# Cross attention: weighed values turned by VectorE in blocks, projections issued in halves, and another split of the copies from PSUM

## What is computed

```python
x = _layernorm(x + _L0_xattn_ref(x, mask_Bx1xSxS_fk0, ctx_2048, L0_xattn_Wq, L0_xattn_Wk, L0_xattn_Wv, L0_xattn_Wo, L0_xattn_gate), axis=-1)
...
q = split_heads(hidden_states @ Wq, q_len)
k = split_heads(hidden_states @ Wk, q_len)
v = split_heads(hidden_states @ Wv, q_len)
...
q = q * cos + _rotate_half(q) * sin
k = k * cos + _rotate_half(k) * sin
scores = jnp.einsum('bhqd,bhkd->bhqk', q, k) * inv_sqrt_d
scores = scores + attention_mask
...
attn_output = jnp.einsum('bhqk,bhkd->bhqd', w, v)
...
a_scores = jnp.tanh(gate) * jax.nn.softmax(a_scores.astype(jnp.float32), axis=-1).astype(q.dtype)
attn_output = attn_output + jnp.einsum('bhqk,bhkd->bhqd', a_scores, a_v)
attn_output = attn_output.transpose(0, 2, 1, 3).reshape(bsz, q_len, hid)
return attn_output @ Wo
```

## Time and profile before

| | |
|---|---|
| three runs, us | 2973.5, 2974.13, 2975.09 (median 2974.13) |
| the profiled execution | 2976.63 us, its span 2974.8 us |
| cross-attention loop | 1713.1 to about 2747 us of the span |
| busy: TensorE, VectorE, ScalarE | 94%, 59%, 47% of the span |
| moved by DMA | 100.10 MB, mean 34 GB/s |

### The profile page before, as it was taken

One profiled execution on the slowest core, in us unless ns is written; L12 is line 12 of the kernel. 1 busy time (PEld: TensorE's weight loads), 2 busy tenths in 40 slices (PEclk: granted clock), 3 DMA queues, 4 the chain that ended last, 5 costly groups with the idle time before them and its releaser, 6 DMA issues. The chain is left out here.

```text
span 2974.8 us, 81892 instructions
## 1 busy us (share of the span) xinstructions
PE 2807.7 (94%) x34646; PEld 1760.9 (59%) x34646; DVE 1748.0 (59%) x4940; ACT 1384.1 (47%) x3313; POOL 503.5 (17%) x626
## 2 busy tenths in 40 slices
...
...
DMA packets 96922, 100.10 MB, mean 34 GB/s; under 512 B 38192, under 2 KB 84528, under 8 KB 95408
## 3 DMA queue, kind: packets, MB, share of 16 engines
...
## 5 line engine op out<-in xcount | busy, mean ns | idle before, releaser
L201 PE MATMUL dr_p<-x_t,dr_w_g 128*128 128x512 f32 x1536 | 740.1, 609 | 11.0 <-DMA dr_w_g<-in_w_in 7.6
L1276 ACT ACTIVATE xa_probs<-xa_probs,xa_low 128x256 f32<-128x256 f32 x1024 | 436.6, 497 | 45.6 <-DVE xa_low L1428 43.6
L201 PEld LDWEIGHTS dr_p<-x_t,dr_w_g 128*128 128x128 f32 x1536 | 268.2, 191 | 226.5 <-issue 216.4
L1428 DVE CUSTOM_DVE_ANT_0 xa_probs<-xa_s,xa_mask 128x256 f32<-128x256 f32 x512 | 213.8, 418 | 263.0 <-PE xa_s L1187 263.0
L1200 PEld LDWEIGHTS xa_t<-ident,xa_probs 128*128 128x128 f32 x2048 | 223.2, 142 | 132.2 <-issue 79.1
L635 DVE SCALAR_TENSOR_TENSOR dr_acc<-dr_p,dr_taps,dr_acc 128x510 f32<-128x510 f32 (+2 forms) x384 | 284.9, 742 | 23.2 <-ACT dr_acc L493 15.2
L1200 PE MATMUL xa_t<-ident,xa_probs 128*128 128x128 f32 x2048 | 286.9, 281 | 7.7 <-DVE xa_probs_t L1437 6.0
L1282 ACT ACTIVATE xa_probs_t<-xa_t 128x512 f32<-128x512 f32 x256 | 152.8, 597 | 250.7 <-PE xa_t L1200 249.1
L1428 DVE CUSTOM_DVE_ANT_0 xa_probs<-xa_s,xa_zeros 128x256 f32<-128x256 f32 x512 | 214.4, 419 | 0.0
L1437 DVE COPY xa_probs_t<-xa_t 128x512 f32<-128x512 f32 x256 | 176.3, 689 | 43.4 <-PE xa_t L1200 29.4
L1215 PE MATMUL xa_o<-xa_probs_t,xa_val 128*32 128x128 f32 x4096 | 140.7, 278 | 44.6 <-DVE xa_probs_t L1437 24.8
...
...
...
## 6 DMA issues: line engine op xcount, KB each, us to landing
...
```

The lines of the kernel that those rows point to most:

```text
L201: mm = pe.matmul(bank[:, :], w_g[:, k, m, :], x_t[:, k, 2 * S * batch:2 * S * (batch + 1)], start=(k == 0), stop=(k == KC - 1))
L1276: op = act.activation(at, at, ACT.Exp, bias=low[:, v % 3, i, kind:kind + 1], scale=-1.0)
L1428: op = dve.tensor_tensor_reduce(out=probs[:, v % 3, i, kind, :], in0=bank_s[i][:, kind * S:(kind + 1) * S], in1=mask[:, par, q, :] if kind ...
```

## The change

norm and turn are no longer pieces of TensorE, and mixed is no longer copied by ScalarE. In each even unit VectorE transposes bank_o (128x512) in blocks of 32x32 into mixed (*turn_mixed*, after the first two tops), which brings 32 queries of each of four head pairs to the rows; it shares out as before, now from SBUF into *joined*, and transposes that (128x128) in blocks into attn_t, the layout that out reads (*share*, at the end of the unit). attn_t has two slots.

The pieces stand in two tables: BETWEEN (between the halves) and BEHIND (behind both). The ten pieces of HALF are issued in two parts, half of their matmuls at one place and half at the next; the bank is waited for at the first part only, and taken after the last. ScalarE copies both bank_t after the first half of turn_probs, VectorE both after the second, each ahead of what followed the copies before. The root moves to unit 7 of a batch, the rate to unit 8. The gate is laid out for the new rows. The diff, cut:

```diff
-        attn = a.sb("attn", [P, 2, D])
-        attn_t = a.sb("attn_t", [P, KC, P])
+        joined = a.sb("joined", [P, 4, 2, XD])
+        attn_t = a.sb("attn_t", [P, 2, XT, P])
...
-        copied = [sem(f"copied{j}") for j in range(2)]
+        copied = [[sem(f"copied{m}{j}") for j in range(2)] for m in range(2)]
...
-        LATE = {0: "x0", 1: "x1", 2: "q0", 3: "q1", 5: "qt0", 6: "ak0", 7: "ak1", 8: "k0", 9: "k1", 10: "v0", 11: "v1",
-                12: "av0", 13: "av1"}
-        EARLY = {7: "qt1", 11: "kt0", 13: "kt1"}
...
+        HALF = {"ak0", "ak1", "q0", "q1", "v0", "v1", "k0", "k1", "av0", "av1", "out0", "out1"}
+        BETWEEN = ("ak0", "ak1", "x0", "count", "q0", "q1", "out1", "qt1", "v0", "v1", "k0", "k1", "av0", "kt1", "av1", "out0")
+        BEHIND = ("ak0", "ak1", "x1", "q0", "q1", "qt0", "out1", "v0", "v1", "k0", "k1", "kt0", "av0", "av1", "spread", "out0")
...
-            if d % 2 == 0:
-                return ("norm", u // 2 - 1) if u else None
-            if d == 9:
-                return "turn", QT * b
-            if d == 1:
-                return ("turn", QT * b - 1) if b else None
-            if d == 15:
-                return ("spread", b - 1) if b else None
-            if d == 3:
-                return ("count", b - 2) if b > 1 else None
-            return (EARLY[d], b + 1) if d in EARLY and b + 1 < B else None
...
+            what = (BEHIND if behind else BETWEEN)[d]
+            use = named(what, b)
+            if not use:
+                return None
+            if what not in HALF:
+                return use, True, True
+            whole = list(itertools.chain.from_iterable(zip(BETWEEN, BEHIND)))
+            is_first = whole.index(what) == 2 * d + behind
+            return use, is_first, not is_first
...
-        BY_DVE = ("qt0", "qt1", "kt0", "kt1", "norm", "out", "count")
+        BY_DVE = ("qt0", "qt1", "kt0", "kt1", "out", "count")
...
-            wait_taken(pe, previous[use])
...
+            if first:
+                wait_taken(pe, previous[use])
...
-                for h in range(2):
+                for h in halves_now:
...
-            elif what == "norm":
-                wait(pe, mixed_taken, at + 1)
-                for n in range(4):
-                    mm = pe.transpose(bank[:, n * P:(n + 1) * P], mixed[:, n * P:(n + 1) * P], ident)
-            elif what == "turn":
-                wait(pe, normed, XT * (at + 1))
-                for k in range(KC):
-                    mm = pe.transpose(bank[:, k * P:(k + 1) * P], attn[:, at % 2, k * P:(k + 1) * P], ident)
...
-                wait_taken(pe, ("turn", at))
-                for k in range(KC):
-                    mm = pe.matmul(bank[:, :], attn_t[:, k, :], w_o[:, k, :], start=(k == 0), stop=(k == KC - 1))
-            mm.then_inc(made, 1)
+                wait(pe, normed, XT * (at + 1))
+                for k in quarters_now:
+                    mm = pe.matmul(bank[:, :], attn_t[:, at % 2, k, :], w_o[:, k, :], start=(k == 0), stop=(k == KC - 1))
+            if last:
+                mm.then_inc(made, 1)
...
-                    if i == 2 and inner(v):
-                        pe_make(pe, inner(v))
+                    if i == 2 and piece(v, 0):
+                        pe_make(pe, *piece(v, 0))
                     wait(pe, exped, 4 * v + i + 1)
-                    wait(pe, copied[i % 2], 2 * v + i // 2)
+                    wait(pe, copied[1 - i // 2][i % 2], v + i // 2)
...
-                if outer(u):
-                    pe_make(pe, outer(u))
+                if piece(u, 1):
+                    pe_make(pe, *piece(u, 1))
...
-            def copy(v, m):
-                wait(act, turned[0], 2 * v + m + 1)
+            def copy(v):
...
-                act.activation(probs_t[:, v % 2, 2 * m].rearrange("p k t n -> p (k t n)"), bank_t[0][:, :], ACT.Copy)\
-                    .then_inc(copied[0], 1)
+                for j in range(2):
+                    wait(act, turned[j], 2 * v + 1)
+                    act.activation(probs_t[:, v % 2, j].rearrange("p k t n -> p (k t n)"), bank_t[j][:, :], ACT.Copy)\
+                        .then_inc(copied[0][j], 1)
...
-                copy(u, 0)
-                if early(u):
-                    act_take(act, early(u))
-                copy(u, 1)
+                copy(u)
+                if ended(u, 0):
+                    act_take(act, ended(u, 0))
                 if u + 1 < LAST:
                     exps(u + 1)
-                if late(u):
-                    act_take(act, late(u))
-                if u % HALVES == 5 and u > HALVES:
+                if ended(u, 1):
+                    act_take(act, ended(u, 1))
+                if u % HALVES == 7 and u > HALVES:
...
-                if u % 2:
-                    g = u // 2
-                    wait(act, weighed, 8 * (g + 1))
-                    if g:
-                        wait(act, made, made_at["norm", g - 1])
-                    act.activation(mixed[:, :], bank_o[:, :], ACT.Copy).then_inc(mixed_taken, 1)
...
+        def turn_mixed(v, g):
+
+            wait(v, weighed, 8 * (g + 1))
+            v.transpose(mixed[:, :], bank_o[:, :]).then_inc(mixed_taken, 1)
+
...
+            for h in range(2):
+                op = v.reciprocal(shares[:, :, h], blocks[:, :, h, :, 1 - h, 0])
...
+            v.tensor_tensor(shares[:, 1], shares[:, 1], gains[:, t, :, None].to_broadcast([P, 2, 4]), ALU.mult).then_inc(norm_step, 1)
...
+            op.then_inc(norm_step, 1)
+            wait(v, norm_step, 4 * g + 3)
+            v.tensor_tensor(joined[:].rearrange("p q h d -> p h q d"), parts[:, 0], parts[:, 1], ALU.add).then_inc(norm_step, 1)
+            if t == 0 and tile >= 2:
+                wait(v, made, made_at["out", tile - 2])
+            wait(v, norm_step, 4 * g + 4)
+            v.transpose(attn_t[:, tile % 2, t, :], joined[:].rearrange("p q h d -> p (q h d)")).then_inc(normed, 1)
...
-            def copy(v, m):
-                wait(dve, turned[1], 2 * v + m + 1)
+            def copy(v):
...
-                dve.tensor_copy(probs_t[:, v % 2, 2 * m + 1].rearrange("p k t n -> p (k t n)"), bank_t[1][:, :]).then_inc(copied[1], 1)
+                for j in range(2):
+                    wait(dve, turned[j], 2 * v + 2)
+                    dve.tensor_copy(probs_t[:, v % 2, 2 + j].rearrange("p k t n -> p (k t n)"), bank_t[j][:, :]).then_inc(copied[1][j], 1)
...
-                    tops(u + 1, 0)
-                copy(u, 0)
-                if early(u):
-                    dve_take(dve, early(u))
-                if u + 1 < LAST:
-                    tops(u + 1, 1)
-                copy(u, 1)
+                    tops(u + 1, 0, 1)
+                if u and u % 2 == 0:
+                    turn_mixed(dve, u // 2 - 1)
+                if ended(u, 0):
+                    dve_take(dve, ended(u, 0))
+                copy(u)
...
-                if late(u):
-                    dve_take(dve, late(u))
-                if u % HALVES == 6 and u > HALVES:
+                if ended(u, 1):
+                    dve_take(dve, ended(u, 1))
+                if u and u % 2 == 0:
+                    share(dve, u // 2 - 1)
+                if u % HALVES == 8 and u > HALVES:
...
+            turn_mixed(dve, LAST // 2 - 1)
+            share(dve, LAST // 2 - 1)
```

89 lines of the change are left out of this document (42 added, 47 removed).

## The result

| | before | after |
|---|---|---|
| four runs each, us | 2971.02 to 2975.09, median 2973.82 | 2886.79 to 2895.5, median 2894.46 |
| ratio, with its 95% interval | | 0.9726 (0.9714 to 0.9738) |
| the profiled execution | 2976.63, span 2974.8 | 2894.66, span 2892.8 |
| mean granted clock of TensorE | 0.982 | 0.981 |

The kernel is 79 us faster. 2888 was forecast, with 2862 to 2926 around it, so the forecast is 6.5 us too low.

A forecast was written before the change was run, and what follows sets the result against it. TensorE was taken to bound the kernel, with 11.3 us of stalls a batch. Gains of 75.6 (seven batches), 9.7 (last batch) and 1.3 (tail) made 86.6: 2976.6 to 2890.0, less 2.5 for the runs' median, 2888; range 2862 to 2926.

The forecast's parts named there:

- The batch, 117.1: Sixteen units of a full batch: 116.3 us plus 0.8 for joints of split pieces, down from 127.9; 75.6 over seven batches.
- The walk: Unit-by-unit reckoning of a full batch: 3.94 us fixed TensorE work plus pieces, later where VectorE or ScalarE is late.
- Ten pieces leave TensorE: 5.1 us: Per batch, eight norm and two turn pieces leave TensorE, 0.51 us each: 5.1 us.
- Unit 6 near 7.6 in place of 10.1: Unit 6 of a batch loses norm's 1.33 us wait on ScalarE's copy mixed, falling from 10.13 to 7.57 us.
- The copies: ScalarE copies both banks after the first half, VectorE after the second; split pieces hide them; light units take 5.8 us.
- The last batch: 9.7 forecast: Last batch, nearly all light units: eight even units gain about 1 us each, the table-change unit some more.
- fewer stalls give it no new cause to fall; I count nothing: TensorE's granted clock, read as 1.00 in batch 5 and two units, stays there: no time counted.
- The tail: 1.3 less forecast: After the last batch, choose ends at 2726.03 as before and the last out starts at 2728.3, not 2729.58.
- Rival A: VectorE's PSUM transpose runs at half pace, 1.4 us not 0.65: 33 us less gain, 2921; chance 0.17.
- Rival B: The walk's own stalls, 4.8 us a batch, vanish as VectorE works ahead in heavy units: 2865; chance 0.09.
- C: VectorE becomes the bound: at 6 us more a pair of units, 128 us slower, 3100; chance 0.03.
- D: Gain undone, within 0.2%: light units wait behind ScalarE's second copy as long as before behind VectorE's; chance 0.03.

The follow-up runs named there:

- turned_twice: The changed kernel with the 128x512 block transpose from PSUM made twice, the first into a scratch tile: 2903.83 us, ratio 0.9774 to the kernel before.
- turn_alone: The changed kernel with VectorE turning and root and rate moved, but pieces whole in their old places and the old copies: 2948.94 us, 0.9932.
- gap_filled: turn_alone with four unread transposes put back where norm stood, in even units with a whole piece behind: 2950.53 us, 0.9918.
- busy_in_wait: The changed kernel with 24 unread TensorE transposes ahead of the weighing in units 0 and 9 of the last batch: 2890.61 us, 0.9725.
- spread_router: The changed kernel with VectorE's choose and rate cut and moved across units, and last values turned ahead of choose: 2886.39 us, 0.9711.

## Why the prediction was right, and where its sizes were off

**TensorE bounds the kernel, with its stalls around it: right.** All that moved the units did so through TensorE's issue, its waits or its clock. VectorE could take 44 us more for some 10 (turned_twice).

**The batch, 117.1: measured 116.67**, so 78.7 for seven batches where 75.6 were forecast. The walk's numbers for the pieces, taken from start to start in the earlier trace rows, hold to a tenth of a microsecond. Unit 0 is half a microsecond longer than forecast: VectorE takes out0, issued in unit 15, and its statistics ahead of choose, which begins 1.14 us after the scores (2183.95 against 2182.81) and not 0.8. Units 1 and 9 are 0.3 and 0.16 shorter, and the 0.8 for the joints is not there: units 1 to 15 last 108.38 together, the walk without it has 108.37. VectorE's busy time rose by 5.4 us a batch and not by 8.

**"Ten pieces leave TensorE: 5.1 us".** As a difference of issue it is right, as a gain it was not one of itself. With the old places (turn_alone) the turning and the moved root and rate give 2.1 us between two full batches (127.9 to 125.8), and four transposes in norm's gap cost nothing (gap_filled). The prediction counted the whole batch anew and so didn't fall into this, but a sum of "removed instructions by duration" would have. The other 59 us come with the new places. Whether the places without the turning would have done it wasn't tried: norm needs the one bank_p between the halves of a split piece.

**Unit 6 near 7.6 in place of 10.1: right in its size** (7.67), by a chain that was read one link short. Norm waited for ScalarE's copy "mixed", but that copy was late because the root stood ahead of it and loaded another table. From ScalarE's timeline of the kernel before:

```profile
2275.02 1.28 ACT L1268 ACT_TABLE_LOAD   x1
...
2276.52 0.58 ACT L1309 ACTIVATE xa_mixed<-xa_o 128x512 f32<-128x512 f32 x1
```

In the first batch, which has no root (and no out before it), unit 6 took 8.79. The change takes the copy off ScalarE and moves the root to unit 7 as well; no run divides the two. In its new place the root costs nothing in a full batch (unit 8 takes 7.49 to 7.50, with it and without it).

**The copies.** That ScalarE's and VectorE's new order is what hides the waits was the forecast's reading; the runs don't bear it out. Swapped back it makes no difference on the old places (2949 and 2950), little on the new ones (2890 and 2894), none with the rate whole in unit 9 (2879 and 2880), and with the rate in unit 11 the old copies are 6 us faster (2880 and 2886). With the new places the traces agree on the sign: a full batch is 0.4 to 0.8 us shorter with the old copies (116.28 and 116.67, 116.09 and 116.79, 114.53 and 115.35). Units 5 and 11 take 6.65 and not 6.88 with them, while unit 9 takes 8.46 and not 7.69. So the gain of heavy units is that of the halves laid between and behind, whoever copies, and the new order of the copies is, if anything, a small loss.

**The last batch: 9.7 forecast, 3.2 measured.** This term failed. It took eight light even units at 1 us less each and 1.7 for the unit with the change of tables; the batch was not walked. The table of this batch shows what it left out.

First, an even unit gained less. Units 2, 10 (at full clock, busy_in_wait) and 12 came from 6.8 to 6.1, so 0.7 and not 1. In such a unit the first half is turned 1.32 after the scores begin (2616.82 to 2618.14) and 1.21 in the odd one after it, and the weighing starts 0.26 after the second copy's end (2621.66 to 2621.92) against 0.14 in the odd one; together that is the difference between 6.11 and 5.88. Why the weighing is later there wasn't tried. It writes the bank that VectorE had just turned, which the forecast left out, but that was done at 2620.21.

Second, work that the change moved lands in light units. The rate, moved to the end of unit 8, now stands ahead of unit 9's copies: 8.16 where it was 5.85, while unit 7, which had borne it, gives back only 0.5. The root in unit 8 leaves that unit at 6.8. Choose, behind out0 and its statistics, makes unit 0 0.6 longer. And out0, moved into unit 15, leaves units 14 and 15 together where they were (13.10 against 13.23). Without rate and choose in these places, in spread_router, unit 9 takes 5.85 and unit 0 7.16.

Third, the clock, though not in the way that "fewer stalls give it no new cause to fall; I count nothing" has it, and hardly as a difference. The clock falls in two units after the change and costs 4.5 us; it falls in units 1, 3 and 13 before (granted 0.64, 0.78 and 0.76), where unit 1 takes 8.23 and in a full batch 5.85, and unit 13 takes 7.13 and its like, unit 11, 5.84. The mean over the batch is 0.94 for both kernels. The prediction had read the clock in one unit of this batch only. By an estimate from these unit times the falls cost the kernel before some 5 us (2.4 in unit 1, 1.3 in unit 13, about 1.5 in unit 3), so at full clock on both sides the gain would have been no larger than 3.2.

**The tail: 1.3 less forecast, 0.8 more measured.** The prediction walked the turning itself right (transpose to out takes 2.57, 2645.06 to 2647.63, where it had 2.3), but kept choose's end where it was before. out0 has moved from unit 14 to unit 15, so VectorE first takes it (2641.01 to 2642.6), and choose is later by that. spread_router, which turns the values ahead of choose, has its last out 4.20 after the weighing: this is the size of what was overlooked, 2.5 us.

**Rival A (a dearer handover) was priced far too high.** A read at 1.4 us in place of 0.7 was to cost 33 us; turned_twice does just that to VectorE's queue, and it costs some 10. The mechanism was right (units 0, 2 and the light even ones pay), the sizes were not: in a full batch 1.3 and not 3.8, in the last about a third of a microsecond in each light even unit and not 0.7 to 0.9. **Rival B** (the walk's stalls vanish) is out: the stalls of units 0, 7, 9 and 10 are there. (Its price doesn't follow either: 4.8 us a batch would be 34 in seven batches and 2854, not 22 to 25 and 2865.) **C** is refuted with turned_twice, **D** by the time.

The Trainium skill, "VectorE: DVE Perf Modes", section "The three transpose paths", gives 311 ns for a block transpose of 128x128 on VectorE, in bf16. The trace has 311 ns for 128x128 in fp32, which agrees. The advice that the prediction puts under this section, to transpose 128x128 on TensorE, stands in "Rules for kernel authors" of the same page. It is for a full transpose; the layout here needed only blocks, and TensorE was the bound.

In sum: 86.6 forecast, 82.0 measured in the span. +3.1 of the batches, -6.5 of the last one and -2.1 of the tail are 5.5 less than forecast, 4.6 of which the spans show. The medians are 6.5 apart because the 2 us that the kernel before's median lay below its profiled execution were taken off, and after the change there is no such distance (2894.46 and 2894.66). That the total came so near owes something to luck: the batches missed on one side, the last batch and the tail on the other.
